# Reordered start of the last feed-forward phase, and shorter runs of row gathers

## What is computed

```python
h = _layernorm(x, axis=-1) * (1 + cb) + sb
logits = hidden @ router_w.T                  # 128 -> 16 experts
top_vals, top_idx = jax.lax.top_k(logits, 1)  # one expert for each token
...                                           # scores = sigmoid(top value)
routed_in = hidden[None, :, :] * scores.T[:, :, None]
gate_up = einsum('nth,nhf->ntf', routed_in, gate_up_proj)      # 128 -> 2 x 128
routed_out = einsum('ntf,nfh->nth', up * silu(gate), down_proj)
shared = silu(hidden @ shared_gate_w.T) * (hidden @ shared_up_w.T) @ shared_down_w.T
x = x + gb * (shared + expert_sum)            # shared: 128 -> 512 -> 128
```

## Time and profile before

| | us |
|---|---|
| median of 3 runs | 1195.31 |
| lowest, highest | 1193.45, 1200.34 |
| the profiled execution | 1193.35 |
| its span, first to last instruction | 1191.5 |
| PE busy | 1047.2 |
| DVE busy | 948.4 |
| ACT busy | 781.1 |
| POOL busy | 317.6 |

### The profile page before, as it was taken

The page is one execution under the profiler, slowest core; times in us unless marked ns, Lnnn a source line. Parts: engine busy times, 40 slices in busy tenths (PEclk is TensorE's granted clock), DMA queues, the critical chain, the costliest instruction groups (busy, mean ns, idle before and its releaser), DMA issues. The chain is left out here.

```text
span 1191.5 us, 23036 instructions
## 1 busy us (share of the span) xinstructions
PE 1047.2 (88%) x8668; PEld 488.8 (41%) x8668; DVE 948.4 (80%) x1457; ACT 781.1 (66%) x1555; POOL 317.6 (27%) x462
## 2 busy tenths in 40 slices
PE   6887599467778999999999999999999998889797
PEld 4675499433321222222222222222222257567555
DVE  7976554459789999999999999999999527756345
ACT  4543134135422999999999999999999966724221
POOL 4622267657530000000000000000000034057263
PEclk9986799768775999999999999999999997989899
DMA  7001277309990022220222202222010003124522
GB/s 235 1 19 54 76 206 200 102 22 190 207 223 14 3 34 35 34 34 3 34 34 35 34 3 34 34 35 34 12 25 2 3 2 132 38 68 115 66 59 82
DMA packets 93972, 76.70 MB, mean 64 GB/s; under 512 B 42884, under 2 KB 72836, under 8 KB 93352
## 3 DMA queue, kind: packets, MB, share of 16 engines
q1 hardware_dynamic: 89000, 65.27, 23.5%
q0 software_dynamic: 4864, 9.97, 4.6%
HBM read 47.74 MB, written 27.39 MB: 63 GB/s over the span
## 5 line engine op out<-in xcount | busy, mean ns | idle before, releaser
L1416 DVE TENSOR_REDUCE mx<-p_psA 128x1 f32<-128x1024 f32 x512 | 585.5, 1217 | 9.3 <-PE p_psA L1575 9.2
L1507 ACT ACTIVATE p_pt<-p_psS 128x512 f32<-128x512 f32 x1024 | 548.2, 596 | 38.0 <-PE p_psS L1597 18.3
L1610 PE MATMUL p_acc<-p_pt,V 128*32 128x256 f32 x4096 | 328.4, 392 | 15.4 <-ACT attn L1498 13.8
L1575 PE MATMUL p_psA<-K,Q 48*128 48x512 bf16 x1024 | 320.0, 395 | 9.3 <-DVE mx L1416 7.8
L1597 PE MATMUL p_psS<-Q,K 51*128 51x512 bf16 x1024 | 310.2, 384 | 0.0
L1610 PEld LDWEIGHTS p_acc<-p_pt,V 128*32 128x32 f32 x4096 | 81.9, 108 | 211.2 <-ACT p_pt L1507 110.5
L1333 POOL TENSOR_TENSOR mr<-zeros,mx 128x16 f32<-128x16 f32 x32 | 7.1, 223 | 547.0 <-DVE mx L1416 547.0
L1575 PEld LDWEIGHTS p_psA<-K,Q 48*128 48x128 bf16 x1024 | 57.0, 94 | 232.9 <-DVE mx L1416 196.2
L1597 PEld LDWEIGHTS p_psS<-Q,K 51*128 51x128 bf16 x1024 | 62.6, 93 | 18.1 <-ACT p_pt L1507 12.6
L1025 DVE TENSOR_TENSOR f_h<-f_bank,b 128x512 f32<-128x512 f32 x40 | 27.7, 692 | 37.5 <-PE f_bank L1089 37.5
L1933 POOL DMA_INDIRECT h<-hrows,gidx x32 | 30.8, 963 | 57.9 <-DMA hrows<-h 46.5
(11 more groups left out here) (318 smaller groups left out, 1419.3 us busy)
## 6 DMA issues: line engine op xcount, KB each, us to landing
f_w<-in_w SPq DMA_DIRECT2D x40, 256.0 KB, 3.5
Q<-q_rows SPq DMA_DIRECT2D x32, 192.0 KB, 4.7
K<-k_rows SPq DMA_DIRECT2D x32, 192.0 KB, 5.2
hrows<-h SPq DMA_DIRECT2D x8, 512.0 KB, 3.2
result<-f_shared_kept SPq DMA_DIRECT2D x12, 256.0 KB, 3.1
result<-f_y SPq DMA_DIRECT2D x10, 256.0 KB, 3.5
V<-v_rows SPq DMA_DIRECT2D x16, 144.0 KB, 5.8
x<-in_x SPq DMA_DIRECT2D x4, 512.0 KB, 5.5
```

The lines of the kernel that those rows point to most:

```text
L1416: dve.tensor_reduce(mx[v % 2][:, h, qt:qt + 1], psA[t][:], AX.X, ALU.max).then_inc(a_max, 1)
L1507: act.activation(pt[s % 2][:, head_at(s, j), :], psS[k % 3][:], ACT.Exp, scale=INV_SCALE).then_inc(s_out, 1)
L1575: mm = pe.matmul(psA[t][:, c * 512:(c + 1) * 512], Q[g % NBUF][rows, pair, q0:q0 + P], K[g % NBUF][rows, pair, c * 512:(c + 1) * 512], sta ...
L1610: mm = pe.matmul(acc[VW * h:VW * (h + 1), cols], V[g % NBUF][:, kc, h * (HD + 1):h * (HD + 1) + VW], pt[s % 2][:, h, cols], start=(kc == 0 ...
```

## The change

The opening, on TensorE: all transposes and logits come first, and the shared products, of which pieces 0 to 3 stood between them, come behind. Pieces 0 and 1 stand ahead of `ranks` (before: 0 to 4), 2 to 6 between `ranks` and `inverse` (before: 5 to 8), 7 to 11 behind it. On ScalarE: `turned(b)` comes ahead of the normalisation, half of batch 2 is normalised on VectorE instead, the exponential comes ahead of all silus, and the rows of the four batches are weighted behind pieces 2, 3, 5 and 6 (before: 4, 5, 7 and 8). On VectorE: `modulate(3)` moves behind `totals`, and the three gates inside the routing move behind it. On GpSimd: the wait for all gathers so far stands ahead of tiles 8, 16, 24, 32 and 40.

```diff
                     q = k // GT
-                    if k == 2 * GT:
-                        for done in range(2):
-                            pool.wait_ge(got[done], 16 * GT)
+                    if k % (2 * GT) == 0 and k:
+                        for done in (q - 2, q - 1):
+                            pool.wait_ge(got[done % len(got)], 16 * GT * (done // len(got) + 1))
...
-                    for i in range(b * TB + (SPLIT if b == B - 1 else 0), (b + 1) * TB):
+                    for i in range(b * TB + (SPLIT if b == B - 1 else TB // 2), (b + 1) * TB):
...
+                turned(0)
                 normalise(2)
-                turned(0)
+                turned(1)
                 normalise(3)
-                turned(1)
-                shared.silu(act, 0)
                 turned(2)
-                shared.silu(act, 1)
                 turned(3)
-                shared.silu(act, 2)
-                shared.silu(act, 3)
                 act.wait_ge(shifted, 1)
                 act.activation(neg[:], neg[:], ACT.Exp).then_inc(exp_done, 1)
+                shared.silu(act, 0)
+                shared.silu(act, 1)
                 act.wait_ge(gate_ready, 1)
-                for b, ks in enumerate(((4,), (5,), (6, 7), (8,))):
+                for b, ks in enumerate(((2,), (3,), (4, 5), (6,))):
                     for k in ks:
                         shared.silu(act, k)
                     weight_rows(b)
-                for k in range(9, EK):
+                for k in range(7, EK):
                     shared.silu(act, k)
...
+                    if b == B - 2:
+                        for i in range(b * TB, b * TB + TB // 2):
+                            ins = dve.tensor_scalar(M.h[:, i, :], M.x[:, i, :], M.mean[:, i:i + 1], M.rstd[:, i:i + 1], ALU.add, ALU.mult)
+                        ins.then_inc(norm_dve, 1)
+                        return
...
+                normalise(B - 2)
                 normalise(B - 1)
                 modulate(0)
                 modulate(1)
                 modulate(2)
-                modulate(3)
...
-                shared.gate(dve, 0)
                 disp.totals(dve, link)
-                shared.gate(dve, 1)
-                shared.gate(dve, 2)
+                modulate(3)
                 disp.positions(dve, link)
...
-                for k in range(3, EK):
+                for k in range(EK):
...
                 turn(0)
                 turn(1)
                 logits(0)
+                turn(2)
+                logits(1)
+                turn(3)
+                logits(2)
+                logits(3)
                 pe.wait_ge(ld_shared, 16 * 2)
                 shared.up(pe, 0)
-                turn(2)
-                logits(1)
                 shared.up(pe, 1)
-                turn(3)
-                logits(2)
-                shared.up(pe, 2)
-                logits(3)
-                shared.up(pe, 3)
-                shared.up(pe, 4)
                 disp.ranks(pe)
-                for k in range(5, 9):
+                for k in range(2, 7):
                     shared.up(pe, k)
                 disp.inverse(pe)
-                for k in range(9, EK):
+                for k in range(7, EK):
                     shared.up(pe, k)
```

More of the change, by code:

```diff
@@ L2121, in turn @@
                     for j in range(2):
-                        if b == B - 2:
+                        if b == B - 2 and j == 0:
+                            pe.wait_ge(norm_dve, 1)
+                        elif b == B - 2:
                             pe.wait_ge(norm_act, 1)
                         elif b == B - 1:
-                            pe.wait_ge(norm_dve, j + 1)
+                            pe.wait_ge(norm_dve, j + 2)
                             if j == 1:
```

## The result

20 executions of each: 1200.19 us after against 1195.53 before (medians; 1194.69 to 1206.11 and 1192.06 to 1200.34). The ratio is 1.0043, 95% interval 1.0029 to 1.0057: slower by 4.7 us. The prediction's sum had 10.7, and its forecast of 1205.0 lay 9.7 above the median then known (1195.31). One later execution of the changed kernel, in g3_after, fell in a slower state (1237.48 us) and is left out of that run's median and ratio. The profiled execution took 1203.27 us, its span is 1201.4.

The account below looks back on a forecast made before the run. It took the last phase's chain of waits (opening, routing, gathers, tail) as the bound. Terms -2.0 + 3.2 + 6.15 + 3.3 = +10.7 us on 1193.35 gave 1204.0; with half the median's 1.96 offset, 1205.0, range 1197 to 1210.

Parts of the forecast that it names:

- my case: The prediction's main case, with half clock on TensorE throughout the opening: 1200 to 1210 us, chance 0.64.
- if the clock is at 1.00 before 1010: Sign of a wrong forecast: TensorE at full clock in the opening before 1010 us, where 0.50 was expected.
- (a): Opening on TensorE: transposes and logits at half clock throughout, last logits at 1021.3 against 1023.83, a gain of 2.5 us.
- (b): Shared pieces 0 and 1 ahead of the counts: counts end at 1030.5, a gain of 2.0 us, bounds 1.0 to 9.1.
- (c): Exponential first on ScalarE, ahead of the silus: nothing gained or lost.
- (e): modulate(3) behind totals on VectorE: a net 0.6 us on the way to the indices, within their slack; no cost.
- (d): Rows weighted on ScalarE behind later pieces: ready 15.6 us after the counts instead of 12.4, a loss of 3.2.
- (f): Stops in the gathers ahead of tiles 16, 24 and 32: 2.05 us each, 6.15 together, bounds 6.0 to 11.0.
- (g): Stop ahead of tile 40: 22.8 us from tile 39's start to the last landing against 19.5, a loss of 3.3.
- (h): Tail after the last landing: the same four tiles and the same 20 shared pieces, no change.
- Rival 2: Gathers: the long run without a stop slows the last ones and stops cure it; +2.6, 1196 to 1198 us, chance 0.10.
- Rival 1: Opening: the clock rises there, before about 1010; +3.6 us in all, 1197 to 1199 us, chance 0.15.

Follow-up runs that it names:

- g3_after: The changed kernel measured again, on another chip: 1222.00 us against 1220.86 for the kernel before, ratio 1.0020.
- e2_reorder: The changed kernel without the added stops (reordered opening, one stop ahead of tile 8): 1217.21 us against 1217.07 for the kernel before, ratio 0.9981.
- e4_best: The changed kernel without added stops, free slots spread over 128 rows, rows weighted one piece earlier: 1214.42 us against 1217.07 for the kernel before, ratio 0.9979.
- g3_rows_first: The changed kernel without added stops, rows weighted one piece earlier, free slots still reading row 0: 1217.83 us against 1220.86 for the kernel before, ratio 0.9965.
- e3_spread: The kernel before with free gather slots reading 128 different rows instead of row 0: 1218.99 us against 1217.07 for the kernel before, ratio 1.0006.
- g3_after_spread: The changed kernel with free gather slots spread over 128 different rows: 1219.88 us against 1220.86 for the kernel before, ratio 0.9997.
- s2_reorder: The changed kernel without the added stops, run once more: 1220.93 us against 1220.26 for the kernel before, ratio 1.0003.
- b2_before: The kernel before, unchanged, profiled on another chip in a group of runs where the kernel before took 1220.26 us.

## Why the prediction was right, and where not

The direction held, and the stops are the loss, as said; the size was twice too large. That 1204.0 was said for the profiled execution and 1203.27 measured is luck: that execution is 3.1 us above its kernel's median, and the terms miss on both sides. The opening is off by -3.0, the rows by -1.4 and the stop ahead of tile 40 by -2.5; the three stops by +1.4, the first gather by +1.2, the tail by +1.7, and 1.6 came ahead of the phase. The median of 1200.19 lies at the very edge of what I called my case, 1200 to 1210, and below the 1201.3 from which I had counted a time as slower.

One sign that I set for being wrong was met: "if the clock is at 1.00 before 1010". It was, up to 1006.7, by a late fall and not by the rise that I had in mind.

- **(a), (b) The opening.** The reading that the logits don't raise the clock was right in eight profiles out of eight. The term that failed is the start: "I take half clock throughout". In the profiled execution the first transposes and logits ran at full clock for 4.6 us. The logits ended at 18.0 from the phase's start instead of 20.8, the counts at 27.0 instead of 30.0. Between the two, (b) has 9.2 and it was 9.0. Where the clock was down from the start, logits and counts were 20.6 and 29.3 to 30.8: that was my case, and it is one of three, not the rule. Counted by the end of the counts, the gain is 5.0 us here, 8.0 in e2_reorder and e4_best, 1.2 to 2.7 where the clock was down from the start: all inside the bounds of (b), 1.0 to 9.1, of which I had taken 2.0, near the low end. (The low bound is mis-summed: 1021.3 + 7.2 for two pieces at half clock + 3.7 is 1032.2, a gain of 0.3.) The gain depends a little on the profile of before as well, whose counts end at 31.9 to 32.8. I worked from one profile of before in which the clock was low at the phase's start. That the same code can enter the phase at either clock could not be read from it.
- **(c), (e)** cost nothing, as said; the indices are ready 16.1 us behind the counts where it was 15.5, the 0.6 of (e). The first gather waits for the store of the rows (43.26 <-DMA hrows<-h) and not for the indices. With the rows one piece earlier, it waits for the indices.
- **(d) The rows.** R + 15.6 to the tenth. The step behind it was mis-sized: I moved the first gather by the whole 3.2, and the store of the last batch, 4.85 us in the earlier trace rows, took some 3.6 here (1044.75 to the gather at 1048.40). From counts to gathers it is 19.3 instead of 17.5: +1.8. Without that order the indices would have been last, some 2 us sooner (16.9 to 17.4 in the three profiles with the earlier rows, 19.2 to 19.3 in the others).
- **First gather.** Not a step of mine: it takes 2.57 us instead of 1.41, so that tile 8 starts 13.8 behind it instead of 12.6. +1.2. g3_rows_first, whose first gather waits for the indices, has 12.8.
- **(f) Three stops.** 2.81 + 3.27 + 2.38 - 3 x 0.30 = 7.6 against 6.15; inside the bounds of 6.0 and 11.0.
- **(g) The stop ahead of tile 40.** The idle 3.71, the step 4.66 instead of 5.2, and then 1122.04 + 6.87 - 1113.30 = 15.6 us for eight tiles instead of 17.6: 20.3 in all against 22.8, a loss of 0.8 where I had 3.3. An empty tile costs 1.24 us of the engines here, where I had 1.57 from seven and a half of the nine tiles; over all nine it is 1.43 in the kernel before. That a stop leaves the 1.88 us for a tile as they are was too simple: by the same reckoning it is (15.6 - 2.6) / 8 = 1.6 here. From the first gather to the last landing it is 80.5 us, +9.7; (f) and (g) together said 9.4. The sum held and its terms did not.
- **(h) The tail** is not unchanged: +1.7, with the clock down for 3.4 us behind a pause of 2.0 us that stood there before.
- **Rival 2** fell with e3_spread and e4_best. **Rival 1** as written, a rise before about 1010, never happened in the new order; a late fall did, and where it came at 9.1 it was worth nearly as much (8.0 of 9.1).

*What remains of the sum.* With the logits' three cases the first gather lies 6.3 or 3.2 us ahead of the 49.5 of before, or 0.6 behind it; with +9.7 from the gathers that gives +3.4, +6.5 and +10.3. The median of +4.7 lies between the first two. That is an argument, not a measurement: two of the three cases come from profiles of other chips, and how often each comes on the first chip was not measured.

*On the other chips* the loss is smaller (1.0020 for the whole change), and the stops alone cost 6.6 and 7.0 us by the medians (0.44 and 0.60% by the ratios) instead of 9.7. There my premise that "GpSimd is the slowest of the three in this stretch" is false: TensorE paces the experts at 6.0 us for four tiles, and a stop of 2 us every eight tiles partly fits in. Why it costs as much as it does there is not settled. The profiles show TensorE at half clock for 20.5 us of its experts' stage in both runs with the stops alone, for 17.0 and 20.4 in the two of the whole change and for 7 to 17 in those without. That could be a clock that falls in the idle of a stop, but the two ranges touch and it was not tried apart.

## What to carry to other kernels

A wait for landings in a loop that the waiting engine paces costs its whole latency each time (2.1 to 3.0 us here); where another engine paces the loop, part of it is hidden. Read first which engine it is, on more than one run, since on another chip it may be another one. A bound on an engine's clock needs the clock at the entry as a case of its own. Removing what delays one input of a start is worth no more than the distance to the next input.

## What the runs showed of the hardware

- Gathers whose 128 indices all name one DRAM row cost 1.2 to 1.6 us of the 16 DMA engines each (1.24 in the profile after, 1.57 in the earlier trace rows), against 0.24 for other rows at the same place (e4_best): five to six times as much. Four kernels with 128 different rows had 9 to 11% of the engines in queue 0 over the last gathers, those with row 0 52 to 75%. The pair that differs in this alone has 52.4 and 9.1% (g3_after, g3_after_spread). On two other chips, where the spread was tried alone, it bought no time that can be told (e3_spread; g3_after_spread is 2.1 us under g3_after, with intervals that overlap). On the first chip, where the chain runs through the last landing, it was not tried.
- TensorE, busy without a gap on transposes and logit products, stayed at 1.2 GHz for 20.6 us (s2_reorder). The Trainium skill (TensorE: Matmul & The Clock Gate, What's actually happening) has activity release the clock; the stretch of s2_reorder does not agree, with 25.98 of 26.00 us busy and the clock at 0.50.
- The same kernel takes 1195 us on one chip and 1217 to 1221 on three others, and the experts' stage accounts for 11 us of it: 70.9 and 82.3 us from the first gather to the last group, with pauses of 2 us in which the other engines seem to wait for TensorE. Another 12 us stand ahead of the phase, whose first transpose is at 1012.8 in b2_before and at 1000.5 in the first profile. The cause is open for both.
